# A separate head for batch 0: x loaded once into the gather ring, the table written first, offsets of six chunks made beside the sampling

## What is computed

```python
def _L0_conv_ref(x, w_off, b_off, w_conv):          # called with x = _gn(x), group norm
    om = conv3x3(x, w_off) + b_off                  # 27 channels
    off = om[:, :2 * K2].reshape(B, K2, 2, Ho, Wo)
    mask = sigmoid(om[:, 2 * K2:])
    ys = off[:, :, 0] + hs + ki;  xs = off[:, :, 1] + ws + kj
    sampled = vmap(_bilinear)(x, ys, xs) * mask[:, None]
    out = einsum('bckhw,ock->bohw', sampled, w_conv)
x = x + _L0_conv_ref(_gn(x), ...)
x = x + _L1_conv_ref(_gn(x), ...)   # q1 = ternary(w1), q2 = ternary(w2), batch norms
```

## Time and profile before

| | us |
|---|---|
| median of 3 runs | 3021.32 (3019.83 to 3022.24) |
| the profiled execution | 3026.24 |
| its span, first to last instruction | 3024.2 |
| first gather | 184.8 |
| sampling of batch 0 (stage 0), first gather to that of batch 1 | 184.8 to 679.5 |

### The profile page before, as it was taken

One profiled execution on the slowest core, in us unless ns is written; L12 is line 12 of the kernel. 1 busy time (PEld: TensorE's weight loads), 2 busy tenths in 40 slices (PEclk: granted clock), 3 DMA queues, 4 the chain that ended last, 5 costly groups with the idle time before them and its releaser, 6 DMA issues. The chain is left out here.

```text
span 3024.2 us, 37569 instructions
## 1 busy us (share of the span) xinstructions
PE 2610.6 (86%) x11674; PEld 1741.7 (58%) x11674; DVE 2101.8 (70%) x4522; ACT 1182.2 (39%) x2039; POOL 1354.2 (45%) x1262
## 2 busy tenths in 40 slices
PE   3668888888999999999999998989999896999940
PEld 2444444444565555556566665555555676999940
DVE  5577778777777778777777776776766434565665
ACT  1234444444444444444444434344443112232345
POOL 1036655664554555545555555555653002333300
PEclk9879999999999999999999999999999998999975
DMA  4679999999898999989899998999997212111169
GB/s 152 176 258 347 368 355 359 344 364 318 318 339 314 338 347 349 326 307 329 315 329 334 336 315 307 329 335 324 334 329 257 94 53 67 53 56 50 51 257 408
DMA packets 277870, 827.35 MB, mean 274 GB/s; under 512 B 25436, under 2 KB 59228, under 8 KB 276964
## 3 DMA queue, kind: packets, MB, share of 16 engines
q0 software_dynamic: 165888, 604.05, 55.0%
q1 hardware_dynamic: 111844, 221.72, 21.2%
HBM read 740.19 MB, written 85.48 MB: 273 GB/s over the span
## 5 line engine op out<-in xcount | busy, mean ns | idle before, releaser
L360 POOL DMA_INDIRECT G<-pixel_pairs,quad_c x1152 | 1190.2, 1033 | 933.2 <-PE psT L785 639.0
L648 DVE SCALAR_TENSOR_TENSOR G<-G,wts_c 128x256 f32<-128x256 f32 (+1 forms) x2304 | 1259.6, 615 | 171.7 <-DMA G<-pixel_pairs,quad_c 166.9
L748 PE MATMUL psD<-ST,wconv 128*128 128x512 f32 x2304 | 1066.8, 609 | 0.0
L748 PEld LDWEIGHTS psD<-ST,wconv 128*128 128x128 f32 x2304 | 433.3, 197 | 451.0 <-issue 451.0
L410 ACT ACTIVATE G<-G,wts_c 128x256 f32<-128x256 f32 x1152 | 489.6, 497 | 419.4 <-DVE G L648 418.7
L737 PE MATMUL psF<-pf,qw 128*128 128x512 f32 x2304 | 629.4, 422 | 14.6 <-DVE pf L570 7.6
L737 PEld LDWEIGHTS psF<-pf,qw 128*128 128x128 f32 x2304 | 428.5, 189 | 163.0 <-issue 54.2
L445 ACT ACTIVATE ST<-psT 128x1024 f32<-128x1024 f32 x288 | 294.5, 1023 | 481.3 <-PE psT L785 481.1
L785 PE MATMUL psT<-idn,G 128*128 128x128 f32 x2304 | 323.8, 287 | 168.1 <-ACT G L410 167.6
L785 PEld LDWEIGHTS psT<-idn,G 128*128 128x128 f32 x2304 | 277.4, 147 | 247.0 <-issue 122.4
L737 PE MATMUL psA<-po,woff 128*64 128x512 f32 x1152 | 346.9, 449 | 6.3 <-DVE po L570 6.3
(11 more groups left out here) (144 smaller groups left out, 1604.1 us busy)
## 6 DMA issues: line engine op xcount, KB each, us to landing
pixel_pairs<-yT SPq DMA_DIRECT2D x112, 256.0 KB
G<-pixel_pairs,quad_c POOLq DMA_INDIRECT x1152, 6.4
xz<-in_x SPq DMA_DIRECT2D x32, 512.0 KB, 7.1
xres<-in_x SPq DMA_DIRECT2D x32, 512.0 KB, 7.0
x<-x1c SPq DMA_DIRECT2D x32, 512.0 KB, 4.9
h<-h1c SPq DMA_DIRECT2D x32, 512.0 KB, 3.8
out<-h SPq DMA_DIRECT2D x16, 1024.0 KB, 17.5
xo<-in_x SPq DMA_DIRECT2D x24, 640.0 KB, 7.0
```

The costliest lines, as they stand in the source:

```text
L360: pool.indirect_dma_start(out=G[:, i % RING, :], out_offset=None, in_=tbl[d.b].rearrange("y x q c -> (y x) (q c)"), in_offset=bass.Indirec ...
L648: dve.scalar_tensor_tensor(g[:, 0:w], g[:, w:2 * w], wts_c[:, d.p, q * NG + i:q * NG + i + 1], g[:, 0:w], ALU.mult, ALU.add).then_inc(d_ma ...
L748: ins = pe.matmul(psD[:, oc, :], wconv[:, t, k, oc * 128:(oc + 1) * 128], ST[:, k % 3, t, :], start=(k == 0 and t == 0), stop=(k == TAPS - ...
```

## The change

Stages -2 and -1 are replaced by a function `head` on each engine, and `schedule` begins with stage 0. In the head the eight chunks of batch 0 are loaded once, into slots 0 to 7 of the ring G (x_all), statistics are taken there, y is made in place, transposed into a ring of four buffers (yt_ring) and written to the table. Offsets are made in the head for chunks 0 and 1 only. Those of chunks 2 to 7 are made in stage 0 while chunks 0 to 5 are sampled (j, two chunks ahead; j2 is the chunk three ahead, which is loaded, normalised and split): 36 matmuls of 64x512 at taps 0 to 3 (J_TAPS) into psF, indices at taps 7 and 8, a load of x into xf. Statistics of batch 1, w1 (in slots 8 to 11 and x1c, three parts) and the first split of batch 1 stand in the head too. Stage 0 writes five chunks out after its loop, so that the loop runs once. The semaphores of batch 0's old o job are raised by hand.

```diff
+            x_all = G[:].rearrange("p s c -> p (s c)")[:, 0:CT * H * W].rearrange("p (t x) -> p t x", t=CT)
+            g_flat = G[:].rearrange("p s c -> p (s c)")
+            W1_SLOT = CT * H * W // (4 * C)
+            raw1 = [(0, 0, 9, g_flat[:, CT * H * W:CT * H * W + 9 * C]), (1, 0, 7, g_flat[:, CT * H * W + 9 * C:CT * H * W + 16 * C]),
+                    (1, 7, 9, x1c[:, 0, :])]
+            above1 = pf[:, 1].rearrange("p q t h w -> p (q t h w)")[:, 0:HW]
+            yt_ring = [ST[:, i].rearrange("p t x -> p (t x)").rearrange("p (t c) -> p t c", t=PT) for i in range(3)] + [yT]
...
-                for s in range(-2, NB + 1):
+                for s in range(0, NB + 1):
...
-                        emit(s, *now, *then)
-                    walk(eng, at, 3)
+                        just = (ahead(r, rh, p, 2), ahead(r, rh, p, 3)) if s == 0 else (None, None)
+                        emit(s, *now, *then, *just)
+                    walk(eng, at, 5 if s == 0 else 3)
+            J_TAPS = {0: [0, 1], 1: [2, 3], 2: [4, 5], 3: [6, 7, 8]}
...
+                for r in range(NR):
+                    sp.dma_start(x_all[:, :, r * PX:(r + 1) * PX], rows_of(x, 0, r * RC, RC)).then_inc(h_load[r], 16)
...
+                def load_j(j):
+                    hold(sp, j_split, j.n - 1)
+                    sp.dma_start(flat(xf[:, j.p, :, j.top:j.top + j.rows, :]),
+                                 rows_of(x, 0, j.y0, j.rows)).then_inc(j_load[j.p], 16)
+
+                def write_table(b, r, src, done):
+                    for h in range(2):
+                        for up in range(2):
+                            dst = tbl[b][ds(r * RC + h + 1 - up, PT, step=2), 1:1 + W, up, :]
+                            sp.dma_start(dst.rearrange("t x c -> x t c"), src[64 * h:64 * h + 64, :, :]).then_inc(done, 16)
+
+                def head():
+                    for t, k0, k1, raw in raw1:
+                        sp.dma_start(raw, w1.rearrange("(t c) k o -> c t (k o)", c=128)[:, t, k0 * C:k1 * C]).then_inc(s_w1, 16)
+                    load_z(Chunk(1, 0, 0, 0, True, False))
+                    load_z(Chunk(1, 1, 0, 1, False, False))
+                    table_border()
+                    for r in range(NR):
+                        sp.wait_ge(h_yt, 2 * (r + 1))
+                        write_table(0, r, yt_ring[r % 4], h_tw[r % 4])
+                        if r == 1:
+                            sp.wait_ge(s_edge, 16 * 4 * NB)
+                            load_j(Chunk(0, 2, 1, 0, False, False))
+                        if 1 <= r < NR - 1:
+                            load_z(Chunk(1, r + 1, (r + 1) // 2, (r + 1) % 2, False, r + 1 == NR - 1))
+                        if r == 2:
+                            sp.dma_start(wconv[:].rearrange("p t k o -> p t (k o)"),
+                                         w_conv.rearrange("(t c) k o -> c t (k o)", c=128)).then_inc(s_wconv, 16)
+                    load_o(Chunk(1, 0, 0, 0, True, False))
...
+                    if j2:
+                        load_j(j2)
                     if o:
                         hold(sp, o_yt, PT * (o.n + 1))
+                        write_table(o.b, o.r, yT, o_tw)
...
+                            for i in range(4):
+                                pool.wait_ge(h_tw[i], TW * NR // 4)
+                            pool.wait_ge(j_split, 2)
+                        else:
+                            hold(pool, o_tw, TW * (d.n + NR) + CREDIT)
+                    hold(pool, o_idx if s else j_idx, d.n + 1)
...
+                def head():
+                    group_sqrt((0, 0))
+                    act.wait_ge(s_gnok, 1)
+
+                    def y_rows(r):
+                        for t in range(CT):
+                            v = x_all[:, t, r * PX:(r + 1) * PX]
+                            i = act.activation(v, v, ACT.Identity, bias=bij[:, t:t + 1], scale=scj[:, t:t + 1])
+                        i.then_inc(h_y, 1)
+
+                    def turned(r):
+                        for u in range(2):
+                            act.wait_ge(h_turn, 2 * r + u + 1)
+                            if r >= 4 and u == 0:
+                                act.wait_ge(h_tw[r % 4], TW)
+                            act.activation(yt_ring[r % 4][:, 2 * u:2 * u + 2, :].rearrange("p t c -> p (t c)"), psT[:, u, :], ACT.Copy).then_inc(h_yt, 1)
+                    for r in range(3):
+                        y_rows(r)
+                    for r in range(NR):
+                        turned(r)
+                        if r + 3 < NR:
+                            y_rows(r + 3)
+                        if r == 4:
+                            jt_om_evac(Chunk(0, 0, 0, 0, True, False))
+                        if r == 5:
+                            jt_om_turned(Chunk(0, 0, 0, 0, True, False))
+                    jt_normalise(Chunk(0, 2, 1, 0, False, False))
+                    jt_om_evac(Chunk(0, 1, 0, 1, False, False))
+                    jt_om_turned(Chunk(0, 1, 0, 1, False, False))
+                    group_sqrt((0, 1))
+                    normalise(Chunk(1, 0, 0, 0, True, False), xo, o_load, sc0, bi0, o_y, (0, 1))
...
+                        if j and k == 4:
+                            jt_om_evac(j)
+                        if j and k == 6:
+                            jt_om_turned(j)
+                        if j2 and k == 6:
+                            jt_normalise(j2)
...
+                def head():
+                    for r in range(NR):
+                        dve.wait_ge(h_load[r], 16)
+                        for t in range(CT):
+                            i = dve.bn_stats(st0[:, t, r, :], x_all[:, t, r * PX:(r + 1) * PX])
+                    i.then_inc(h_stat, 1)
+                    dve.wait_ge(h_stat, 1)
+                    norm_moments((0, 0), st0)
+                    norm_variance((0, 0))
+                    norm_scale((0, 0), scj[:], bij[:])
+                    j0, j1, j2 = Chunk(0, 0, 0, 0, True, False), Chunk(0, 1, 0, 1, False, False), Chunk(0, 2, 1, 0, False, False)
+                    dve.wait_ge(h_y, 2)
+                    jt_split(j0, x_rows(0, 9))
+                    dve.wait_ge(s_w1, 48)
+                    weight_sums(0, raw1[0][3])
+                    take_stats(Chunk(1, 0, 0, 0, True, False))
+                    weight_sums(1, raw1[1][3])
+                    step(weight_sums(2, raw1[2][3]))
+                    weight_sums_ready(3)
+                    dve.wait_ge(h_y, 3)
+                    jt_split(j1, x_rows(7, 10))
+                    take_stats(Chunk(1, 1, 0, 1, False, False))
+                    jt_indices(j0, 0)
+                    jt_indices(j0, 1)
+                    weight_extremes(0)
+                    weight_limits(0)
+                    compare_w1(0)
+                    take_stats(Chunk(1, 2, 1, 0, False, False))
+                    take_stats(Chunk(1, 3, 1, 1, False, False))
+                    compare_w1(1)
+                    compare_w1(2)
...
+                    i.then_inc(s_tern, 1)
+                    jt_split(j2, xf_rows(j2))
+                    jt_indices(j1, 0)
+                    jt_indices(j1, 1)
+                    for r in range(4, NR):
+                        take_stats(Chunk(1, r, r // 2, r % 2, False, r == NR - 1))
+                    dve.wait_ge(z_stat, 2 * NR + CREDIT)
+                    norm_moments((0, 1), st0)
+                    norm_variance((0, 1))
+                    norm_scale((0, 1), sc0[:], bi0[:])
+                    split(Chunk(1, 0, 0, 0, True, False), xo, po, o_y, o_hi, o_split, o_conv)
...
-                            indices(o, k - 7)
+                            o_indices(o, k - 7)
+                        if j and k in (7, 8):
+                            jt_indices(j, k - 7)
+                        if j2 and k == 7:
+                            jt_split(j2, xf_rows(j2))
...
+                def jt_conv(j, tap):
+                    if tap == 0:
+                        pe.wait_ge(j_split, j.n + 1)
+                        need(pe, j_omc, j.n)
+                    dy, dx = tap // 3, tap % 3
+                    for t in range(CT):
+                        for part in range(2):
+                            ins = pe.matmul(psF[0:64, 0, :].rearrange("p (h w) -> p h w", h=RC), woff[:, t, tap, :],
+                                            pf[:, 0, part, t, dy:dy + RC, dx:dx + W],
+                                            start=(tap == 0 and t == 0 and part == 0), stop=(tap == TAPS - 1 and t == CT - 1 and part == 1))
+                    if tap == TAPS - 1:
+                        ins.then_inc(j_conv, 1)
...
+                    group_sums((0, 0))
+                    pe.wait_ge(s_woff, 1)
+                    for r in range(3):
+                        turn(r)
+                    for tap in range(4):
+                        jt_conv(j0, tap)
+                    turn(3)
+                    for tap in range(4, TAPS):
+                        jt_conv(j0, tap)
```

(19 more changed lines are left out.)

191 lines of the change are left out of this document (127 added, 64 removed).

## The result

| | us |
|---|---|
| before, median of 4 runs | 3021.78 (3019.83 to 3026.1) |
| after, median of 4 runs | 2999.87 (2997.46 to 3004.02) |
| ratio, 95% interval | 0.9926, 0.9911 to 0.9941 |
| the profiled execution of after, its span | 2997.46, 2995.7 |

The change takes 22 us off, where 50 were forecast; the time lies 3 us above the end of the range. The head did what the forecast said. The sampling of batch 0 gave back twice what was allowed for it. One run further down, of the kernel with DVE's part moved, took 3176.8 us at a granted clock of 0.82 instead of 0.95, and is left out of that kernel's median.

The account below looks back on a forecast made before the run. It took a chain with nothing full to bound the head and gathers to pace stage 0; -80 for the head and +30 for stage 0 made -50, 3021.3 to 2971 us, own range 2958 to 2982, full range 2946 to 2997.

Parts of the forecast that it names:

- The head: Before stage 0: one stage replaces two, first gather at 108 us, first weighted sum at 116; 80 us off, range 62 to 86.
- what was allowed for it: Stage 0, sampling of batch 0 with offsets of chunks 2 to 7 added: +30 us, 5.5 a chunk for six, less 3.
- the loop's turn: Stage 0, at 380 us: the loop runs once instead of twice, so DVE's idle 5.7 us there goes: -3 us.
- Rival 3: Head gains less, x at the rate of paced loads and landings behind table writes: -62, 2989 us; chance 0.12.
- not both in full, since the gathers wait once for both: 3.7 together: Stage 0, each chunk with added work: late work on DVE and PE costs 3.7 us together.
- DVE's lump: Stage 0, taps 7 and 8: a split and a set of indices, 6.9 us of work, costing up to 4 a chunk.
- PE's part: Stage 0, taps 0 to 3: 36 wide and four small matmuls, 10.7 us of work, costing up to 3.4 a chunk.
- bound of +48 from above: Stage 0: upper limit from the row with 72 wide matmuls, 6 x 8.5 - 3 = +48 us.
- PE late at taps 1 to 3 and DVE at 7, 8: Rival 2, stage 0 as slow as the heaviest row: +48, 2989 us; chance 0.18.
- The bytes: Stage 0: one more load of 655 KB a chunk, 1.8 us at 357 GB/s, all of it counting.
- rival 1: Stage 0: the convolution hides and only bytes count, PE's clock speaking for it: +8, 2949 us; chance 0.17.
- signs against it: Changed kernel's profile: a head ending after 130 us, or a chunk under 64 or over 70, would show the forecast wrong.

Follow-up runs that it names:

- kernel with DVE's part moved: Changed kernel, all work kept; batch 0's indices moved to taps 3 and 4 of the next chunk, split to tap 5, normalisation to tap 3: 2965.45 us.
- kernel with nothing added in stage 0: Changed kernel without the stage 0 work for chunks 2 to 7 (load, normalisation, split, convolution, indices), sampled with offsets of chunks 0 and 1: 2934.21 us.
- PE's part alone: Changed kernel without DVE's splits and indices for chunks 2 to 7 in stage 0; loads, ACT's work and convolution kept: 2969.74 us.
- DVE's part alone: Changed kernel without PE's convolution for chunks 2 to 7 and ACT's copies of it in stage 0; loads, splits and indices kept: 2964.15 us.
- spread kernel: Changed kernel, all work kept; convolution at taps 4 to 8, result read at taps 0 to 2 of the next chunk, split at 3, indices at 4 and 5: 2952.71 us.

## Why the prediction was wrong

**The head: right, step by step.** Constants at 17, measured 16.7. Weights and statistics of batch 0: the weights were forecast at the 5.6 us of before and took 2.2, since the CAST of woff took 0.41; hence a scale at 31.5 instead of 36. The wait for the offsets before the indices was forecast at 2.5 and was 1.66. The tie between SP and DVE is there: the last two statistics wait 2.86 and 4.83 us for loads, and the last two table writes go out at 89.66 and 94.24, forecast from 95. First gather and first weighing came 4 us earlier than forecast, 81 and 86 us earlier than before. The kernel with nothing added in stage 0 measures the head in time: 3021.8 - 2934.2 = 87.6, of which 2.6 to 5.7 are the loop's turn, so 82 to 85 for the head where the term was 80. Rival 3, a head that gives less, is out. One small slip is in the working: behind 39.4, the pieces 2.8, 14.9, three statistics of 1.3 and 2.5 make 63.5 and not 62.9, and the kernel has two statistics there and not three.

**Stage 0: the step that failed is "not both in full, since the gathers wait once for both: 3.7 together".** Against 22 us for six chunks by that step, the two parts cost 60.5 (33.0 + 27.5, each measured alone). Three things are in it.

The first is the word once. Before it is applied, the prediction has 4.0 a chunk for DVE's lump and 3.4 for PE's, 7.4 or 44 for six; taking half of that put 22 us at nothing, with no row behind it. DVE's heap stands at taps 7 and 8, PE's at taps 0 to 3: they are reached one after the other, and each holds back transposes and with them the refilling of slots. The two together cost their sum (65.7 against 63.0). That the DMA engines cannot make up the loss between them is an inference; they were at 0.96 to 0.97, and the most that a run reached with this head was 368 GB/s against 359. The DMA share fell to 0.87 where "a little under 0.96" was forecast. No run puts both heaps at the same taps, so whether the gathers would then wait once is not shown.

The second is a term of PE's part put at nothing. Its 3.4 is a price for the heap alone, and the heap alone measured 19.6/6 = 3.3. But the convolution costs 2.2 a chunk (13.4 for six) when it is spread as well, and the prediction has nothing for that. DVE's lump cost 4.6 a chunk (27.5/6), where 4.0 was taken. So the price of a late lump, 3.3 us for 5.7, was about right, though it was read from single chunks; the run that writes the loop out does not settle it (2.6 to 5.7 us for 5.7).

The third is the bound of +48 from above, which stage 0 broke. Its 8.5 a chunk does not follow from the two terms beside it (7.5, and DVE's 3.4 more), and its row says nothing of a place. The 72 matmuls of the second convolution stand in a stage where they are laid among the taps otherwise. The same work as in this change costs 65.7 at its place and 18.5 when spread, so a length can only bound work at the same place. Of the rivals, the second, "PE late at taps 1 to 3 and DVE at 7, 8", named what happened, and its +48 was still short of the 59 by which stage 0 grew (553.8 - 494.8); both figures have the loop's turn taken off.

**The bytes** were oversized: 1.8 us a chunk forecast, 11 in all, with the reason that a DMA share of 0.96 leaves nothing; 2.5 in all measured, not clear of nothing.

**The loop's turn**, 3 in the forecast, is 5.7 by the medians and 2.6 by the length of stage 0; no error can be told.

**The sum, as measured:** -87.6 head and turn, +2.5 loads, +33.0 PE's part, +27.5 DVE's part, +2.7 for the two together, is -22. As forecast: -80, -3, +11, +22 for both, is -50. With 60.5 for the two heaps and its other terms as they were, the forecast would have been -12, or 3010, 10 us above what was measured: the bytes, 8.5 too dear, and the head with the turn, 4.6 too small a gain, erred the other way and made up for a part of the heaps. That the time came out only 3 us above the range is luck to that extent.

**The clock (rival 1).** The granted clock in stage 0 was 0.94 before and is 0.93 to 0.95 in the chunks with 36 more matmuls: on the whole next to nothing was paid back. Taken apart, from 165 to 500, it is 0.92 with nothing added, 0.94 in the change, 0.98 with PE's part alone, though in its heap, 0.90 with DVE's part alone, in which PE waits most for weighed samples (58.4 us against 45.3 with nothing added), and 0.98 in the spread kernel. So the added matmuls did raise the clock, and DVE's heap took it down. That agrees with what the Trainium skill says (TensorE: Matmul & The Clock Gate, section on the HAM clock gate), that activity releases the clock. It did not make the rival come true: at 0.98, PE's part alone still cost 33.0 us.

**What the prediction named as signs against it** came out so: chunks of over 70 us were one, and they are 71 to 73.5. DVE's wait for gathers, forecast to fall from 9 us a chunk, is 11. The last two chunks, which have no added work and were forecast at 62, took 65.6 and 64.5 (61.7 and 63.5 before); why is open.

## What to carry to other kernels

Where a ring of buffers is fed by DMA engines that are nearly full, work added to the engines that empty it is priced first by where it stands in their order, and not by its length or by the engine's share of idle time: 17.6 us of work a chunk cost 11 in two heaps and 3 when each engine's piece was laid at taps where that engine had little else. Heaps on two engines at different taps cost their sum. Before such a change is judged, lay the added pieces into the order tap by tap on every engine, each away from the older work of the same engine, and bound a price only by rows in which the work stands at the same place. When several late lumps are priced and only one is counted, that needs a row of its own.

## What the runs showed of the hardware

- A DMA share of 0.96 was not full: with six more loads of 655 KB the share went from 0.97 to 0.98 and the rate from 359 to 368 GB/s, and the time grew by 2.5 us, not clear of nothing, where their bytes at 357 GB/s are 11.
- One turn of a loop with a long body left DVE idle for 5.72 us and cost 2.6 us of stage 0, or 5.7 (2.7 to 8.2) of the whole time, on a path that gathers set.
- The same CAST of 128x486 took 3.84 us in the kernel before, starting at 8.52, and 0.41 us in the changed one, starting at 17.78. In both kernels GpSimd clears two buffers of 128x5280 until 12.05. In the kernel before with stage 0 written out, the constants came 0.87 us earlier and the CAST took 0.87 us longer. GpSimd's timeline before, then DVE's before and with stage 0 written out:

```profile
3.10 4.51 POOL L340 MEMSET po<- 128x5280 f32 x1
7.54 4.51 POOL L341 MEMSET pf<- 128x5280 f32 x1
```

```profile
8.52 3.84 DVE L466 CAST woff<-ST 128x486 fp32r<-128x486 f32 x1
```

```profile
7.65 4.71 DVE L466 CAST woff<-ST 128x486 fp32r<-128x486 f32 x1
```

The long CAST ends at 12.36 in both, 0.3 us after the second clearing, whenever it begins, and the short one begins after both clearings. So the CAST ended with GpSimd's work and not after a length of its own. The MEMSET of woff just before it took 1.02 us in all three kernels, beside GpSimd's clearing or not.
